# Decoder layer on one core: the last two pipeline steps get orders of their own on TensorE, ScalarE and VectorE

## Chip, cores and metric

The kernel runs on one core of a Trainium2 chip. The metric is the device time of one execution in microseconds, the median of the runs shown. Its engines are TensorE (PE, with its weight loads as PEld), VectorE (DVE), ScalarE (ACT), GpSimd (POOL) and SyncE (SP, which issues the large DMAs). Each engine works through its own instructions in the order in which they are written; between engines only semaphores order the work.

## What is computed

Eight batches of 512 tokens with 512 features pass three layers, each followed by a layer norm: a retention (a decaying sum over time, a linear map, a convolution of 5 taps), an mLSTM attention against a context, and a mixture of 32 experts. The part that matters here is the attention's end, the norms behind it, and the router:

```python
# attention, per batch, 8 heads of 64
log_D = cs[:, :, None] - cs[:, None, :] + ig[:, None, :]      # masked: lower triangle
D_mat = jnp.exp(log_D - max_log_D)
C = qk * D_mat
normalizer = jnp.maximum(jnp.abs(C.sum(-1, keepdims=True)), jnp.exp(-max_log_D))
h = jnp.einsum('hst,htd->hsd', C / (normalizer + EPS), vh)
h = layernorm(h) * ln_scale
x = layernorm(x + h)
# router, over all 4096 tokens
ri = jnp.concatenate([xf, stats(xf)], -1)     # stats: mean, std, min, max, l2, share of tiny values
h = jax.nn.gelu(ri @ r1_w.T + r1_b, approximate=False)
probs = jax.nn.softmax(h @ r2_w.T, -1)
topp, topi = jax.lax.top_k(probs, 2)
idx = jnp.argsort(-score, axis=0)[:cap].T     # each expert takes its 160 best of ALL tokens
```

Because each expert picks its tokens from all batches, nothing of the experts can start before the router's result of the last batch.

## The kernel before

**The pipeline.** The first third of the time is a software pipeline over the eight batches. `run_pipeline` calls `step` for n = 0 to 9 on each engine. In step n three things are interleaved: batch n's retention, first norm and gates (flag `a`, n < 8), batch n-1's attention (flag `s`), and batch n-2's two norms and router (flag `r`). So step 8 (`n.off == NB`) has the attention of batch 7 and the norms and router of batch 6, and no batch of its own; step 9 has only the norms and router of batch 7. The order is written out by hand in one `step` per engine, for TensorE, ScalarE, VectorE and GpSimd; steps 8 and 9 use the same list with the missing parts left out.

**Attention of a batch**, by pairs of heads j = 0 to 3. TensorE `broadcast_max(b, h)` (L545 on, two bf16 matmuls, L556 and L557) writes a head's maxima to the bank `Bb`; ScalarE `decays(b, h)` (L1017) takes their exponential into `Dm[h // 2 % 2]`, and waits for `values` of the pair that used that buffer before, two pairs back. TensorE `scores(b, j)` (L656) makes q times k; VectorE `weigh(b, j)` (L1233) multiplies them into `Dm`. `broadcast_decay(b, j)` (L567) also writes `Bb`, and VectorE `scale_queries(b, j)` (L1242) reads it. TensorE `values(b, j)` multiplies by the values (L672) and adds the earlier chunks' state (L683); VectorE `head_out(b, j)` (four small operations and L1293) divides and writes to `x2`. Since `Bb` is one bank, every broadcast waits for the reader of the one before.

**Norms and router of a batch.** VectorE `norm2_stats` (L1300 to L1308), `norm3_sum` (L1316) and `norm3_stats` (L1323, L1327), with a power on GpSimd after the first (`rstd2`) and after the last (`shift3`); ScalarE `norm3_out` (L933), then `squares` (L943); TensorE `router_in` transposes the four tiles (L700), ScalarE `router_1` copies them out (L1031); VectorE `router_extreme` (L1378), `router_sparse` (L1369) and `router_stats` (L1385 to L1390); GpSimd `roots`; TensorE `router_stats` (L712), `router_hidden` (L718), `router_hidden_stats` (L723); ScalarE copies (L1037) and the Gelus `router_2` (L1042); TensorE `router_logits` (L730); ScalarE `router_3` copies the logits (L1047); VectorE `softmax_1` (L1395, L1397) subtracts the maximum; ScalarE `router_4` takes the exponential (L1052); VectorE `softmax_2` and `top_two` (L1402 to L1433) end with the semaphore step `save`. The selection behind it (DVE L1538 on) waits for `save` of batch 7.

The last lines of the steps on ScalarE and VectorE are these:

```python
                if r:
                    router_4(n - 2)          # ScalarE, L1123: waits for softmax_1 of the same batch
...
                if r:
                    softmax_1(n - 2)         # VectorE, L1516
                if a:
                    weigh(n, 0)
                if n.off == NB + 1:
                    softmax_2(n - 2)
                    top_two(n - 2)
```

`softmax_2` and `top_two` of a batch otherwise come one step later, behind the third norm's statistics. GpSimd's `selection_tables` (L1845 on), constants for the selection, stand at the end of step 8 behind `roots`.

## Time and profile before

| | |
|---|---|
| median of 3 runs | 1753.62 us (1751.96 to 1753.97) |
| profiled execution | 1756.21 us, span on the core 1754.4 us, mean granted clock 0.926 |
| busy over the span | PE 86%, PEld 66%, DVE 43%, ACT 28%, POOL 18% |
| step 8 | from about 545 to 597 us of the span |
| step 9 | 597 to 640.5 us |
| selection and lists | 640.5 to about 750 us |
| experts | about 750 us to the end |

Times in the trace are us from the span's start, and durations us, unless marked ns. A row of the timeline merges successive instructions of one kind (x4: four of them); the bracket at its end gives how long the engine had been idle before and what released it. The ends of matmuls are modelled. PEclk is the granted clock of TensorE as a share of 2.4 GHz: 0.50 is 1.2 GHz.

### The profile page before, as it was taken

Reading aid. Unit: us, or ns where it says so; the run is one execution under the profiler, and the core shown is the slowest. Engines: PE = TensorE matmul, PEld = TensorE weight load, DVE = VectorE, ACT = ScalarE, POOL = GpSimd, SP = SyncE. Lnnn points to the kernel's source line nnn. Section 1 sums busy time; section 2 is a strip of 40 time slices with the busy share of each in tenths; the row PEclk is TensorE's granted clock in tenths of the full one; section 3 lists DMA queues with packets and bytes.
Section 4 is the critical chain, followed back from the end, with each engine's and each line's share of the span. In section 5 each row is a group of like instructions: output and inputs, shape, how many; then the busy total and the mean of one; then the engine's idle time right before and its main releaser. Section 6 shows DMA issues by size and latency. Waiting matters only on the chain.

```text
span 1754.4 us, 28619 instructions
## 1 busy us (share of the span) xinstructions
PE 1504.7 (86%) x11038; PEld 1158.6 (66%) x11076; DVE 758.7 (43%) x1783; ACT 486.9 (28%) x1165; POOL 309.4 (18%) x399
## 2 busy tenths in 40 slices
PE   3589999899897540389999999999999999999995
PEld 2256656556555420278787888878788887878884
DVE  7458999999978569811111111111111111111143
ACT  3446666676664220011111110111111011111123
POOL 3101121111111200011121212112121211212125
PEclk9698998998997765589999999999999999999998
DMA  5203123133211054046776767676776767677696
GB/s 156 72 1 115 48 79 104 48 90 95 75 49 49 1 202 169 0 156 214 285 246 259 264 222 282 214 283 240 264 264 226 278 215 278 239 271 257 230 344 209
DMA packets 92191, 311.02 MB, mean 177 GB/s; under 512 B 42455, under 2 KB 46557, under 8 KB 82781
## 3 DMA queue, kind: packets, MB, share of 16 engines
q1 hardware_dynamic: 78876, 287.87, 44.8%
q0 software_dynamic: 13248, 22.29, 5.6%
q8 instruction: 39, 0.64, 0.1%
q14 instruction: 28, 0.22, 0.0%
HBM read 273.18 MB, written 36.96 MB: 177 GB/s over the span
## 4 chain that ended last, share of the span: by engine, by line
PE 71%; DVE 18%; issue 6%; ACT 3%; DMA 1%; POOL 1%; SPq 0%; DVEq 0%; POOLq 0%; ACTq 0%
PE bank L869 36%; PE banks L881 15%; PE bank L582 5%; PE banks L884 4%; DVE arena L1212 3%; DVE arena L1587 2%; PE banks L672 2%; PE bank L718 1%; PE bank L584 1%; DVE arena L1202 1%; PE banks L683 1%; PE banks L656 1%; DVE arena L1378 1%; PE bank L642 1%; DVE arena L1233 1%
## 5 line engine op out<-in xcount | busy, mean ns | idle before, releaser
L869 PE MATMUL bank<-arena 128*128 128x160 f32 x4608 | 636.0, 300 | 0.7 <-issue 0.7
L869 PEld LDWEIGHTS bank<-arena 128*128 128x128 f32 x4608 | 628.3, 191 | 7.3 <-issue 7.3
L1144 ACT ACTIVATE arena<-bank 128x160 f32<-128x160 f32 x288 | 87.4, 303 | 835.2 <-PE bank L869 835.2
L1748 DVE TENSOR_TENSOR arena<-arena,bank 128x160 f32<-128x160 f32 x256 | 82.3, 322 | 459.4 <-ACT arena L1144 408.8
L881 PE MATMUL banks<-arena 128*128 128x512 f32 x576 | 255.6, 598 | 8.9 <-DVE arena L1750 8.9
L1914 POOL DMA_INDIRECT acc_rows<-arena,keep x64 | 102.8, 1606 | 651.9 <-DVE arena L1693 634.1
L881 PEld LDWEIGHTS banks<-arena 128*128 128x128 f32 x576 | 106.9, 190 | 138.6 <-issue 132.5
L1691 DVE TENSOR_SCALAR arena<-banks,keep 128x512 f32<-128x512 f32 x32 | 24.0, 750 | 318.8 <-PE banks L884 316.6
L582 PE MATMUL bank<-arena 128*128 128x512 f32 x256 | 121.7, 620 | 30.8 <-DVE arena L1212 30.8
L582 PEld LDWEIGHTS bank<-arena 128*128 128x128 f32 x256 | 49.8, 200 | 85.1 <-issue 77.1
L1212 DVE SCALAR_TENSOR_TENSOR arena<-arena 128x512 f32<-128x512 f32 x128 | 96.1, 750 | 3.4
L1017 ACT ACTIVATE arena<-bank,arena 128x128 f32<-128x128 f32 x256 | 72.5, 370 | 43.1 <-PE bank L557 43.1
L884 PEld LDWEIGHTS banks<-arena 128*32 128x32 f32 x2304 | 60.9, 110 | 24.3 <-issue 24.3
L672 PE MATMUL banks<-arena 128*128 128x96 f32 x512 | 71.6, 300 | 2.3 <-DVE arena L1293 2.3
L672 PEld LDWEIGHTS banks<-arena 128*128 128x128 f32 x512 | 68.7, 214 | 7.2 <-issue 7.2
L1902 POOL DMA_INDIRECT arena<-x_rows,keep x64 | 64.2, 1003 | 36.4 <-POOL keep L1894 26.6
L884 PE MATMUL banks<-arena 128*32 128x128 f32 x2304 | 69.5, 274 | 0.0
L1894 POOL COPY keep<-keep 128x2 int32 (+1 forms) x64 | 29.3, 458 | 204.9 <-DVE keep L1682 119.3
L718 PE MATMUL bank<-arena 128*128 128x512 f32 x128 | 60.7, 618 | 0.7 <-ACT arena L1031 0.7
L814 PE MATMUL bank<-arena 128*128 128x1 f16 x30 | 5.6, 185 | 59.2 <-DVE arena L1587 59.2
L1130 ACT ACTIVATE arena<-banks 128x512 f32<-128x512 f32 x32 | 19.1, 597 | 118.7 <-PE banks L850 114.9
L718 PEld LDWEIGHTS bank<-arena 128*128 128x128 f32 x128 | 23.9, 197 | 30.9 <-issue 29.5
(252 smaller groups left out, 1632.9 us busy)
## 6 DMA issues: line engine op xcount, KB each, us to landing
arena<-in_wup SPq DMA_DIRECT2D x32, 4096.0 KB, 12.5
arena<-in_wdn SPq DMA_DIRECT2D x32, 2048.0 KB
arena<-in_aup SPq DMA_DIRECT2D x32, 512.0 KB, 11.7
arena<-in_xT SPq DMA_DIRECT2D x8, 1024.0 KB, 5.3
arena<-in_kT SPq DMA_DIRECT2D x8, 1024.0 KB, 7.2
arena<-in_v SPq DMA_DIRECT2D x32, 256.0 KB, 7.8
x_rows<-arena SPq DMA_DIRECT2D x8, 1024.0 KB, 4.4
acc_rows<-arena SPq DMA_DIRECT2D x8, 1024.0 KB, 6.7
```

The source lines that it names most:

```text
L582: pe.matmul(w[:, :], ST[b.slot][:, c, rows], WT[:, c, :], start=(c == 0), stop=False)
L672: pe.matmul(Pp[:, r * T + tb * PVN:r * T + (tb + 1) * PVN], Dm[j % 2][:, r * T + tb * P:r * T + (tb + 1) * P], va[b.slot][:, tb, h * VW:h ...
L718: pe.matmul(Wb[k][:, :], r1x[:, c, k * P:(k + 1) * P], x2T[:, c, :], start=(c == 0), stop=False)
L869: m = pe.matmul(u[:, g * CAP:(g + 1) * CAP], w, xeT[:, c, :], start=(c == 0), stop=(c == C - 1))
L881: m = pe.matmul(Yb[0][:, :], hact[:, j, 0:P], w, start=(j == 0), stop=(j == J))
L884: m = pe.matmul(Yb[1][CAP2 * c:CAP2 * (c + 1), 0:P], hact[:, j, P:CAP], w[:, c * P:(c + 1) * P], start=(j == 0), stop=(j == J))
L1017: m = act.activation(d[:, tb * P:(tb + 1) * P], Bb[:, tb * P:(tb + 1) * P], ACT.Exp, bias=gcol[b.slot][:, tb, h:h + 1])
L1144: act.activation(sg[k], Ub[k][:, 0:CAP], ACT.Silu).then_inc(up_a(f"silu{j}"), 1)
L1212: dve.scalar_tensor_tensor(row, xT[:, c, k:k + T], cw[:, c, k:k + 1], row, ALU.mult, ALU.add).then_inc(re_v(f"tap{i}_{c}"), 1)
L1748: dve.tensor_tensor(hact[:, j, :], sg[k], u, ALU.mult).then_inc(up_v(f"mul{j}"), 1)
L1902: pool.indirect_dma_start(out=xg[e.slot][:, cols], out_offset=None, in_=rows, in_offset=bass.IndirectOffsetOnAxis(ap=idx_g[e.slot][:, k:k ...
L1914: pool.indirect_dma_start(out=rows, out_offset=bass.IndirectOffsetOnAxis(ap=idx_s[e.slot][:, k:k + 1], axis=0), in_=yy[e.slot][:, cols], i ...
```

## The change

Steps 8 and 9 get lists of their own, `last_values` (step 8, on TensorE, ScalarE and VectorE) and `last_rows` (step 9, VectorE). In step 8 the scores of pair 1 come ahead of the decay and the values of pair 0, the broadcasts and values of batch 7 come ahead of batch 6's router on all three engines, and batch 6's hidden layer and logits come behind `values(b, 3)`. VectorE does batch 6's `norm3_sum` and `norm3_stats` between parts of the attention, and its extremes, counts and statistics around `head_out(b, 3)`. Batch 5's `softmax_2` and `top_two` and batch 6's `softmax_1` move from step 8 to step 9, behind the statistics of batch 7's third norm; batch 6's `softmax_2` and `top_two` go behind batch 7's `router_stats`. On ScalarE, batch 5's `router_4` moves from the end of step 7 to behind `decays(b, 3)`; batch 6's `router_4` is the last of step 8. A 1-element activation on a new tile `tab` with the function Gelu, and one with Exp, stand ahead of the places in steps 8 and 9 where the tables change. In step 9 TensorE does both halves of `router_hidden` ahead of `router_stats`. GpSimd's `selection_tables` move from the end of step 8 to its beginning. The semaphore steps of `softmax_1` move from `ro_v` to `so_v`, since their order among the others is now different.

```diff
@@ -277,6 +277,7 @@
         wsum = room.take(TB)
+        tab = room.take(2)[0:1, 0:1]
@@ -329,9 +330,8 @@
         ro_a = steps("router_scalar", [f"x{tb}" for tb in range(TB)] + ["st", "h0", "h1", "lg", "exp"])
-        ro_v = steps("router_vector", ["extr0", "extr1", "cnt", "msq", "var", "stats",
-                                       "lmax", "lsub"])
-        so_v = steps("softmax_vector", ["lsum", "lrec", "prob", "top", "at",
+        ro_v = steps("router_vector", ["extr0", "extr1", "cnt", "msq", "var", "stats"])
+        so_v = steps("softmax_vector", ["lmax", "lsub", "lsum", "lrec", "prob", "top", "at",
                                        "sum2", "rec2", "oh", "ohs", "save"])
@@ -731,8 +731,38 @@
+            def last_values(b, p):
+                broadcast_max(b, 2)
+                broadcast_max(b, 3)
+                scores(b, 1)
+                broadcast_decay(b, 0)
+                broadcast_max(b, 4)
+                values(b, 0)
+                broadcast_max(b, 5)
+                scores(b, 2)
+                broadcast_decay(b, 1)
+                broadcast_max(b, 6)
+                values(b, 1)
+                broadcast_max(b, 7)
+                broadcast_decay(b, 2)
+                scores(b, 3)
+                broadcast_decay(b, 3)
+                values(b, 2)
+                router_in(p, False, (0, 1))
+                values(b, 3)
+                router_in(p, False, (2, 3))
+                router_hidden(p, 0)
+                router_hidden(p, 1)
+                router_stats(p, False)
+                router_hidden_stats(p)
+                router_logits(p)
             def step(n, a, s, r, x1, x2):
+                if n.off == NB:
+                    last_values(n - 1, n - 2)
+                    return
                 if s:
@@ -782,8 +812,11 @@
                 if r:
+                    if n.off > NB:
+                        router_hidden(n - 2, 1)
                     router_stats(n - 2, a)
-                    router_hidden(n - 2, 1)
+                    if n.off < NB:
+                        router_hidden(n - 2, 1)
                     router_hidden_stats(n - 2)
@@ -1022,11 +1055,12 @@
-            def router_1(b, before):
-                act.wait_ge(*ro_t.at("h1", b - 1))
-                if before:
-                    act.wait_ge(*n1_a.at(f"out{TB - 1}", b + 2))
-                for tb in range(TB):
+            def router_1(b, before, tiles=range(TB)):
+                if tiles[0] == 0:
+                    act.wait_ge(*ro_t.at("h1", b - 1))
+                    if before:
+                        act.wait_ge(*n1_a.at(f"out{TB - 1}", b + 2))
+                for tb in tiles:
                     act.wait_ge(*ro_t.at(f"x{tb}", b))
@@ -1043,16 +1077,41 @@
                 act.wait_ge(*ro_t.at("lg", b))
-                act.wait_ge(*ro_v.at("lsub", b - 1))
+                act.wait_ge(*so_v.at("lsub", b - 1))
                 act.activation(lg, Wb[0][:, 0:TB * NE].rearrange("p (a e) -> p a e", a=TB), ACT.Copy)\
...
+            def table(f):
+                act.activation(tab, tab, f)
+            def last_values(b, p):
+                decays(b, 2)
+                decays(b, 3)
+                router_4(p - 1)
+                for h in range(4, NH):
+                    decays(b, h)
+                norm3_out(p)
+                router_1(p, False, (0, 1))
+                squares(p)
+                router_1(p, False, (2, 3))
+                table(ACT.Gelu)
+                router_stats(p)
+                router_2(p, 0)
+                router_2(p, 1)
+                table(ACT.Exp)
+                router_3(p)
+                router_4(p)
             def router_4(b):
-                act.wait_ge(*ro_v.at("lsub", b))
+                act.wait_ge(*so_v.at("lsub", b))
                 act.activation(pr, pr, ACT.Exp).then_inc(ro_a("exp"), 1)
...
+                if n.off == NB:
+                    last_values(n - 1, n - 2)
+                    return
                 if s:
@@ -1097,6 +1156,8 @@
                     gates_1(n)
+                if n.off > NB:
+                    table(ACT.Gelu)
                 if r:
@@ -1110,12 +1171,14 @@
                     gates_g(n)
+                if n.off > NB:
+                    table(ACT.Exp)
                 if r:
...
                     first_state(n)
-                if r:
+                if r and n.off != NB - 1:
                     router_4(n - 2)
@@ -1170,7 +1233,7 @@
-            for t in (xT[:, :, 0:PAD], xT[:, :, PAD + T:], wgq, wgk, wgv, gm, Fr[0], Fr[1], stT, r1s, bfs[0], bfs[1], zeros):
+            for t in (xT[:, :, 0:PAD], xT[:, :, PAD + T:], wgq, wgk, wgv, tab, gm, Fr[0], Fr[1], stT, r1s, bfs[0], bfs[1], zeros):
                 dve.memset(t, 0.0)
@@ -1392,10 +1455,10 @@
                 dve.wait_ge(*so_v.at("save", b - 1))
-                dve.tensor_reduce(nmx, lg, AX.X, ALU.max).then_inc(ro_v("lmax"), 1)
-                dve.wait_ge(*ro_v.at("lmax", b))
+                dve.tensor_reduce(nmx, lg, AX.X, ALU.max).then_inc(so_v("lmax"), 1)
+                dve.wait_ge(*so_v.at("lmax", b))
                 dve.tensor_tensor(pr, lg, nmx.unsqueeze(2).to_broadcast([P, TB, NE]), ALU.subtract)\
-                    .then_inc(ro_v("lsub"), 1)
+                    .then_inc(so_v("lsub"), 1)
@@ -1436,8 +1499,53 @@
+            def last_values(b, p):
+                norm2_stats(p)
+                scale_queries(b, 0)
+                weigh(b, 1)
+                norm3_sum(p)
+                head_out(b, 0)
+                scale_queries(b, 1)
+                norm3_stats(p)
+                weigh(b, 2)
+                head_out(b, 1)
+                scale_queries(b, 2)
+                weigh(b, 3)
+                scale_queries(b, 3)
+                head_out(b, 2)
+                router_extreme(p, 0)
+                head_out(b, 3)
+                router_extreme(p, 1)
+                router_sparse(p)
+                router_stats(p)
+            def last_rows(b):
+                norm2_stats(b)
+                norm3_sum(b)
+                norm3_stats(b)
+                softmax_2(b - 2)
+                top_two(b - 2)
+                softmax_1(b - 1)
+                router_extreme(b, 0)
+                router_extreme(b, 1)
+                router_sparse(b)
+                router_stats(b)
+                softmax_2(b - 1)
+                top_two(b - 1)
+                softmax_1(b)
+                softmax_2(b)
+                top_two(b)
             def step(n, a, s, r, x1, x2):
+                if n.off == NB:
+                    last_values(n - 1, n - 2)
+                    return
+                if n.off == NB + 1:
+                    last_rows(n - 2)
+                    return
                 if r:
@@ -1516,9 +1624,6 @@
                     weigh(n, 0)
-                if n.off == NB + 1:
-                    softmax_2(n - 2)
-                    top_two(n - 2)
@@ -1863,6 +1968,8 @@
+                if n.off == NB:
+                    selection_tables()
                 if r:
@@ -1879,8 +1986,6 @@
                     gate_chunks(n)
-                if n.off == NB:
-                    selection_tables()
```

## Rows read from the trace of the kernel before

**Rows 1.** Stages: length; busy PE, PEld, DVE, ACT, POOL; granted clock; DMA share, GB/s.
```profile
545.00:597.20 52.20, 39.52 (x228) 28.99 (x230) 34.10 (x92) 19.37 (x51) 10.62 (x27) 0.77 0.11 41
597.20:640.60 43.40, 17.61 (x57) 9.73 (x57) 26.45 (x90) 13.21 (x28) 6.11 (x9) 0.67 0.13 49
```

**Rows 2.** VectorE's timeline, step 8: start, us, operation, [idle <-releaser].
```profile
549.23 2.74 DVE L1308 SCALAR_TENSOR_TENSOR arena<-arena 128x512 f32<-128x512 f32 x4
...
554.66 0.55 DVE L1242 TENSOR_TENSOR arena<-arena,bank 128x384 f32<-128x384 f32 x1
...
565.33 4.47 DVE L1378 TENSOR_REDUCE arena<-arena 128x4 f32<-128x2048 f32 x2
...
572.48 0.17 DVE L1390 TENSOR_SCALAR arena<-arena 128x4 f32<-128x4 f32 x1
...
595.62 0.17 DVE L1284 SCALAR_TENSOR_TENSOR arena<-banks,arena 128x8 f32<-128x8 f32 x1 [3.02 <-PE banks L683]
...
596.47 0.69 DVE L1293 TENSOR_TENSOR arena<-banks,arena 128x512 f32<-128x512 f32 x1
```

**Rows 3.** ScalarE's timeline at the start of step 8 and inside it.
```profile
545.30 0.31 ACT L1052 ACTIVATE arena<-arena 128x128 f32<-128x128 f32 x1 [4.42 <-DVE arena L1397]
...
557.82 1.14 ACT L1017 ACTIVATE arena<-bank,arena 128x128 f32<-128x128 f32 x4 [9.07 <-PE bank L557]
```

**Rows 4.** TensorE's timeline in step 8, at either clock.
```profile
564.75 2.08 PE L656 MATMUL banks<-arena 64*128 64x128 f32 x16
566.76 3.73 PE L672 MATMUL banks<-arena 128*128 128x96 f32 x16
570.41 1.55 PE L683 MATMUL banks<-arena 64*128 64x65 f32 x12
...
572.30 0.63 PE L557 MATMUL bank<-arena 128*128 128x512 bf16 x1
...
592.75 2.00 PE L672 MATMUL banks<-arena 128*128 128x96 f32 x16
594.69 0.89 PE L683 MATMUL banks<-arena 64*128 64x65 f32 x12
```

**Rows 5.** Stretches of 4 us (columns as in Rows 1).
```profile
568.00:572.00 4.00, 4.00 (x25) 3.71 (x25) 4.00 (x8) 0.00 (x0) 0.00 (x0) 0.50 0.45 167
...
620.00:624.00 4.00, 3.38 (x6) 1.11 (x4) 2.77 (x12) 0.00 (x0) 1.18 (x2) 0.75 0.16 60
```

**Rows 6.** GpSimd's timeline in step 8.
```profile
549.28 0.79 POOL L1807 TENSOR_SCALAR arena<-arena 128x4 f32<-128x4 f32 x1 [18.50 <-DVE arena L1304]
...
575.37 3.68 POOL L1771 TENSOR_SCALAR_AFFINE_SELECT arena<-arena 128x128 f32<-128x128 f32 x10
```

**Rows 7.** VectorE's timeline, step 9 and the end of the router.
```profile
597.60 2.46 DVE L1300 BATCH_NORM_STATS2 arena<-arena 128x6 f32<-128x512 f32 x4
...
608.57 0.38 DVE L1327 BATCH_NORM_AGGREGATE arena<-arena 128x2 f32<-128x6 f32 x4
...
614.22 4.48 DVE L1378 TENSOR_REDUCE arena<-arena 128x4 f32<-128x2048 f32 x2 [1.57 <-ACT arena L933]
...
636.72 0.29 DVE L1402 TENSOR_REDUCE arena<-arena 128x4 f32<-128x128 f32 x1 [1.01 <-ACT arena L1052]
...
640.22 0.29 DVE L1433 TENSOR_TENSOR keep<-arena 128x128 f32<-128x128 f32 x1
```

**Rows 8.** ScalarE's timeline, step 9.
```profile
610.89 0.81 ACT L933 ACTIVATE arena<-arena 128x512 f32<-128x512 f32 x1 [12.87 <-POOL arena L1819]
...
630.16 1.28 ACT L1042 ACT_TABLE_LOAD   x1 [3.76 <-PE bank L723]
```

**Rows 9.** TensorE's timeline, step 9.
```profile
617.44 5.94 PE L718 MATMUL bank<-arena 128*128 128x512 f32 x8 [0.69 <-ACT arena L1031]
625.18 0.60 PE L712 MATMUL bank<-keep,arena 128*6 128x128 f32 x4 [1.80 <-issue]
625.62 3.61 PE L718 MATMUL bank<-arena 128*128 128x512 f32 x8
```

## Prediction

> **What bounds the kernel now.** I read the busy time by stage first. In step 8 TensorE is busy 39.5 of 52.2 us at a mean clock of 0.77, VectorE 34.1; in step 9 TensorE is busy 17.6 and VectorE 26.5 of 43.4 [rows 1]. No engine is full in either: both are chains of one batch across four engines, so it is the order of the chain that counts. Behind step 9 stands the selection, which waits for `save` of batch 7 at 640.51 (the end of the last of rows 7), and the experts wait for it in turn. No operation behind `save` is changed, so what `save` gains or loses, the kernel gains or loses. The forecast is therefore one number: when `save` of batch 7 comes.
>
> Then the timelines of each engine, followed backwards from `save`. Step 9 is batch 7 alone and cannot start before its `head_out(b, 3)` at 597.16, which had waited 3.02 us for TensorE [rows 2]; the reader is to see there that in step 8 TensorE does batch 6's hidden layer and logits ahead of batch 7's last values. The change takes that work off batch 7's way in step 8 and puts other work on its way in step 9. I lay out both chains.
>
> **Step 8, laid out anew.** It starts where VectorE ends `norm2_stats(6)`, at 551.97 [rows 2]; this is the same in both kernels. ScalarE has by then no debts: at the end of step 7 it sat 4.42 us waiting for batch 5's `softmax_1` before its exponential [rows 3]. With `router_4` moved behind `decays(b, 3)`, both decays are done by about 544.9 in place of 548.8, but VectorE is in `norm2_stats` until 551.97 anyway, so this gain is hidden; it is worth nothing at the end.
>
> Prices, from rows. At the low clock: a broadcast is two matmuls of 512 columns, L557 at 0.63 and one ahead of it that it overlaps by half: 0.95; scores 2.08, 2.0 on the chain; values from 566.76 to 571.96, 5.15 on the chain [rows 4]. At the high clock: values from 592.75 to 595.58, 2.8 [rows 4]. A decay broadcast is one matmul of three quarters of the columns of L557, hence 0.5 [rows 4]. Decays of one head 1.14 [rows 3], `scale_queries` 0.55 and `head_out` from 595.62 to 597.16, 1.54 [rows 2]. Each hand-over costs some 0.05, which I put into the items.
>
> I take the low clock from the start, because TensorE stands idle for most of the stretch in which VectorE does `norm2_stats(6)`. The new list then gives a chain that hardly ever waits for VectorE's norms: `scale_queries(0)` to 552.5; broadcast 4 to 553.5; values 0 to 558.65; decays 4 (they need the buffer that values 0 frees) to 559.85; broadcast 5, scores 2, decay broadcast 1 to 563.3; `scale_queries(1)` to 563.85; broadcast 6 to 564.8; values 1 to 569.95; decays 6, broadcast 7, decays 7 to 573.25; decay broadcast 2, scores 3, decay broadcast 3 to 576.2; values 2 to 581.35. All of VectorE's `norm3_sum`, `norm3_stats` and `weigh` lie beside it. Then `router_in(p, False, (0, 1))`, which stands between values 2 and values 3: two tiles of transposes, at most 2.0 since they are eight matmuls of the width of scores. That is 583.35. Values 3 costs 2.8 or 5.15; TensorE has worked since 573.3 with almost no break, and before it rose in such a stretch, so I take 3.4: 586.75. `head_out(b, 3)` ends at 588.3, against 597.16: **8.9 us earlier**. With 5.15 for values 3 it is 590.05.
>
> **What now stands on batch 7's way.** (1) VectorE does `router_extreme(p, 1)`, `router_sparse(p)` and `router_stats(p)` of batch 6 between `head_out(b, 3)` and `norm2_stats(7)`: half of 4.47, plus the rest up to the end of the last statistic at 572.65, 2.85 [rows 2]: +5.1 us. Before, only `softmax_1(6)` stood there, from 597.16 to 597.60: -0.45. (2) The three norm pieces take 11.35 (597.60 to 608.95) [rows 7] in both. (3) Before, ScalarE began `norm3_out(7)` at 610.89, 1.94 behind 608.95, released by GpSimd's `shift3` [rows 8]. Now `router_4(6)` stands ahead of it on ScalarE's queue. It waits for `softmax_1(6)`, and that stands on VectorE behind `softmax_2(5)` and `top_two(5)`, 3.8 us (the same operations for batch 7: 636.72 to 640.51) [rows 7]. So `norm3_out(7)` starts 3.8 + 0.65 + 0.35 = 4.8 behind the third norm in place of 1.94: **+2.85 us**. This is the new wait of this change: everything behind `router_4(6)` on ScalarE is held, first `norm3_out(7)`, and for that wait TensorE's transposes and VectorE's extremes. Of batch 5's softmax only the 1.94 us of GpSimd's work lie in cover.
>
> Sum to the start of `norm3_out(7)`: 588.3 + 5.1 + 11.35 + 4.8 = 609.55, against 610.89: **1.35 us earlier**.
>
> **The tail of step 9.** Before, statistics were ready for TensorE at 625.18 (L712), and the second half of the hidden layer came behind them [rows 9]. The first half takes 5.94, partly at the low clock; the second, at the high clock, 3.6 [rows 9]. Both halves first, on the old time axis: from 617.44 they end at 626.9, so L712 goes then and not at 625.18. It takes 0.5; ScalarE's copy of its 512 columns takes at most the 0.81 of an activation of that size [rows 8], say 0.6; and half of L723, two matmuls of 512 columns where a hidden half has eight in 3.6, takes 0.9. The first Gelu's input stands at 629.0, against 630.16 when ScalarE left its wait for it [rows 8]: **-1.15 us**. The Gelu table load of 1.28 [rows 8] goes into ScalarE's wait for statistics: before it had idled 3.76 us right ahead of the load [rows 8] and more ahead of that: **-1.3**. If that cover were gone, 1.28 would be back on the path. The Exp table load ran beside `softmax_1` and held the exponential for part of VectorE's 1.01 us wait at 636.72 [rows 7]; the exponential itself is 0.31 plus hand-overs, so **-0.65**; it now lies beside the logits. Batch 6's `softmax_2` and `top_two` (3.8) lie between `router_stats(7)` and `softmax_1(7)`, a stretch in which VectorE waits some 10 us for TensorE and ScalarE: nothing. Together -3.1. If the first half of the hidden layer meets a clock that is already high, up to 1 more.
>
> A rule of the Trainium skill on the tables: in our rows the load is 1.28 and the first Gelu follows at once [rows 8]. The Trainium skill, "ScalarE: Activation LUTs", section "What ACT_TABLE_LOAD costs", puts a switch of sets at about 2.66 us, since it counts a drain of 1.38 with the load. By the page the two preloads would hide up to 1.4 us more each; no row here shows such a drain on the path, and the sum goes by 1.28.
>
> **Edits at nothing.** `selection_tables` first in step 8: the ten selects that make most of it take 3.68 us, and GpSimd had stood idle 18.5 us before `rstd2(6)` at 549.28 [rows 6]; the tables wait only for batch 7's decay rows, ready by then, so they end near 545.5. If they were late, `rstd2(6)` would hold `norm3_sum(6)`, which now has 2 us of slack behind `weigh(b, 1)`. The stores of batch 6's rows start some 13 us later than at 563, those of batch 7 a little earlier; nobody waits for them before the selection. One more `memset` of one element at the start: under 0.1. The renamed semaphore steps cost nothing.
>
> **Sum.** -1.35 - 3.1 = -4.45, or -5.45 with a first hidden half at the high clock; errors of hand-overs are about 1 either way. I take -5.3, because the hand-laid chain, put to the old order in the same way, comes out about half a us later than the trace. On the profiled execution of 1756.21 that is 1750.9; that execution lies 2.6 above the median of the runs, so on the median it is **1748.3**.
>
> **The rivals.** *Early high clock.* What TensorE's clock does in step 8 is the largest open term. TensorE worked from 568 to 572 without a pause, all value products, at 0.50 [rows 5]; in hidden-layer matmuls of 512 columns the clock went up inside 620 to 624 (0.75) [rows 5]. The new list has broadcasts and scores in a row at 559.9 to 563.3; if the clock rises there or one run of values later, values 1 and 2 save 2.35 each, the broadcasts, scores 3 and transposes about 2.2, values 3 another 0.6: about -7.5 on top, **1740.8**. For it: fewer long pauses from 559.9 on than before. Against it: pauses of 1.1 us at every decay, and half the time is value products, during which it stayed low.
>
> *Low to the end.* The clock stays low through values 3, and hand-overs cost a bit more, or a preload does not take its load off the path (the change doing less than it says; 1.3 and 0.65). Then `head_out(b, 3)` ends at 590.05 and the sum is -4.45 + 1.75 = -2.7, and without the Gelu preload -1.4; I name the middle: **1751.5**, within 0.2%.
>
> *The other batch's router comes late* (slower than before). `router_4(6)` holds `norm3_out(7)` until the logits of batch 6 are there. In my layout these are copied at about 602 to 603, and VectorE asks for them at 609.2: 6.5 us of slack. If the clock also stays low through both hidden halves, they take about 6.9 each (5.94 with a part at the high clock [rows 9]) from 592 on, and end at 606; statistics, L723 and logits at the low clock take 10 more: 616. `norm3_out(7)` then starts at 617.1, 6.2 later than before; less the tail's 3.1, +3.1: **1756.7**. It decides from logits later than 609.2 on. Against it: the row in which just these matmuls raised the clock [rows 5]. The Trainium skill, "TensorE: Matmul & The Clock Gate", section "Part 1: The HAM clock gate (the "warmup" mystery)", has a clock that is halved after idling and comes back after sustained work; by that rule an order that splits TensorE's work into short pieces with waits between them, as this one does at every decay, speaks against the change. The row of 568 to 572 shows more than the page says: even unbroken work left it low.
>
> **How the numbers follow.** The forecast 0.60 (its own range 1746.3 to 1750.5), early high clock 0.22, low to the end 0.14, late router 0.04. About 0.2%, 3.5 us, is what a measurement of this kernel can tell from no change. Faster by more: all of the early clock and nine tenths of the forecast, 0.76, and 0.02 of the third, 0.78; within: 0.18; slower: 0.04. The range must keep the early clock's middle and the third case: 1740.5 to 1751.5.
>
> **What the profile after would show.** `head_out(b, 3)` of batch 7 ending near 588 (582 with the early clock); VectorE's extremes, counts and statistics between it and the second norm, 5.1 us; `norm3_out(7)` released by the exponential of batch 6 (or by VectorE's L1397) and no longer by GpSimd, 4.8 behind the third norm; no table load between L723 and the Gelus of step 9; the exponential of batch 7 right behind `softmax_1`; `save` near 635; everything behind it as long as before. I am wrong if the selection or the first expert takes longer in reaction, if TensorE's clock path differs, or if ScalarE's queue blocks elsewhere.

## The result and the profile after

| | before | changed kernel |
|---|---|---|
| median | 1754.4 us (20 runs) | 1751.87 us (20 runs) |
| ratio to the kernel before | | 0.998, 95% interval 0.997 to 0.9989 |
| profiled execution | 1756.21 us, span 1754.4 | 1749.58 us, span 1747.7 |

The forecast was -5.3 us and 1748.3, from a median before of 1753.62. The ratio says -3.5 us, between -1.9 and -5.3, which on that median is 1750.1; the two medians of the table, taken as they stand, differ by 2.5. In the two profiled executions the span is 6.7 us shorter. Two slow executions are left out of the ratios: one of the kernel before beside b1 and b2 (1797.68 us at a mean clock of 0.886) and one of the six of b2 (2380.34 us at 0.732). The page of the changed kernel (span; busy time, share and count of each engine; the chain of waits by engine) is almost the old one; the gain is not to be seen in shares:

```profile
span 1747.7 us, 28624 instructions
...
PE 1506.6 (86%) x11038; PEld 1159.1 (66%) x11076; DVE 758.2 (43%) x1784; ACT 488.8 (28%) x1169; POOL 309.9 (18%) x399
...
PE 70%; DVE 20%; issue 5%; ACT 3%; DMA 1%; POOL 0%; SPq 0%; DVEq 0%; POOLq 0%; another core or an unknown queue 0%; ACTq 0%
```

The timeline of VectorE in the changed kernel answers to rows 2 and 7. In order: `weigh(7, 0)`, with which I let step 8's chain begin in all kernels; `head_out(7, 0)`; the end of `head_out(7, 3)`; the first extreme after it; the first and the last operation of the second and third norm of batch 7; batch 6's `softmax_1`; the extremes of batch 7; the operation that gives `save`.

```profile
544.27 1.22 DVE L1296 SCALAR_TENSOR_TENSOR arena<-banks,arena 128x1024 f32<-128x1024 f32 x1
...
557.50 0.17 DVE L1347 SCALAR_TENSOR_TENSOR arena<-banks,arena 128x8 f32<-128x8 f32 x1 [2.20 <-PE banks L683]
...
584.51 0.69 DVE L1356 TENSOR_TENSOR arena<-banks,arena 128x512 f32<-128x512 f32 x1
...
585.12 2.28 DVE L1441 TENSOR_REDUCE arena<-arena 128x4 f32<-128x2048 f32 x1
...
590.15 2.47 DVE L1363 BATCH_NORM_STATS2 arena<-arena 128x6 f32<-128x512 f32 x4
...
601.12 0.38 DVE L1390 BATCH_NORM_AGGREGATE arena<-arena 128x2 f32<-128x6 f32 x4
...
605.62 0.29 DVE L1460 TENSOR_TENSOR arena<-arena 128x128 f32<-128x128 f32 x1
...
609.48 4.48 DVE L1441 TENSOR_REDUCE arena<-arena 128x4 f32<-128x2048 f32 x2 [3.57 <-ACT arena L966]
...
633.54 0.29 DVE L1496 TENSOR_TENSOR keep<-arena 128x128 f32<-128x128 f32 x1
```

The chip ran the stages in the order that the prediction lays out: after `head_out(7, 3)` (585.20) come 4.95 us of batch 6's statistics, the norms end at 601.50, and the next thing on the way is batch 6's `softmax_1`, not GpSimd's shift. ScalarE's timeline shows this (answer to rows 8): the exponential of batch 6 released by L1460 (`softmax_1`), `norm3_out(7)` right behind it; then the Gelu table load in a wait, the two Gelus, the Exp table load, the exponential of batch 7:

```profile
605.95 0.31 ACT L1108 ACTIVATE arena<-arena 128x128 f32<-128x128 f32 x1 [6.94 <-DVE arena L1460]
...
606.16 0.80 ACT L966 ACTIVATE arena<-arena 128x512 f32<-128x512 f32 x1
...
615.11 1.28 ACT L1085 ACT_TABLE_LOAD   x1
...
625.12 0.69 ACT L1076 ACTIVATE arena<-bank,arena 128x512 f32<-128x512 f32 x1 [1.28 <-PE bank L723]
...
626.69 1.28 ACT L1085 ACT_TABLE_LOAD   x1
...
629.69 0.31 ACT L1108 ACTIVATE arena<-arena 128x128 f32<-128x128 f32 x1 [0.68 <-DVE arena L1460]
```

TensorE's timeline (answer to rows 4 and 9): values 1, values 2, the transposes of two tiles, values 3, then in step 9 both hidden halves in one piece, the statistics, L723.

```profile
563.71 3.57 PE L672 MATMUL banks<-arena 128*128 128x96 f32 x16
...
567.21 1.55 PE L683 MATMUL banks<-arena 64*128 64x65 f32 x12
...
575.08 3.18 PE L672 MATMUL banks<-arena 128*128 128x96 f32 x16
578.18 0.89 PE L683 MATMUL banks<-arena 64*128 64x65 f32 x12
579.00 1.09 PE L700 MATMUL bank<-keep,arena 128*128 128x128 f32 x8
580.80 2.00 PE L672 MATMUL banks<-arena 128*128 128x96 f32 x16 [0.71 <-DVE arena L1356]
582.73 0.89 PE L683 MATMUL banks<-arena 64*128 64x65 f32 x12
...
612.71 10.08 PE L718 MATMUL bank<-arena 128*128 128x512 f32 x16 [0.69 <-ACT arena L1065]
...
622.62 0.60 PE L712 MATMUL bank<-keep,arena 128*6 128x128 f32 x4
...
623.90 1.98 PE L723 MATMUL bank<-arena 128*128 128x512 f32 x4 [0.68 <-ACT arena L1071]
```

Five lengths describe each kernel; all are differences of two rows of its timelines, as those above. "Start" is the start of `weigh(7, 0)`; step 8 goes from there to the end of `head_out(7, 3)`; "norms" to the last statistic of batch 7's third norm; "hold" from there to the start of `norm3_out(7)`; "tail" from its end (3.2 behind its start) to `save`; "sum" from start to `save`.

| kernel | start | step 8 | norms | hold | tail | sum |
|---|---|---|---|---|---|---|
| before | 545.18 | 51.98 | 11.79 | 1.94 | 26.41 | 95.33 |
| changed | 544.27 | 40.93 | 16.30 | 4.66 | 24.47 | 89.56 |
| changed, again (c_after) | 549.17 | 40.86 | 16.29 | 4.67 | 24.43 | 89.44 |
| e1_norm_first | 545.75 | 42.87 | 16.30 | 1.95 | 24.40 | 88.72 |
| e2_no_preload | 548.96 | 43.29 | 16.30 | 4.79 | 24.89 | 92.48 |
| e3_step9_only | 544.60 | 49.87 | 11.79 | 1.94 | 23.59 | 90.40 |
| e4_filler | 543.08 | 31.35 | 16.29 | 4.67 | 24.13 | 79.64 |
| e5_before_filler | 543.73 | 48.05 | 11.79 | 1.94 | 26.41 | 91.40 |
| e6_filler_norm_first | 546.08 | 34.81 | 14.10 | 1.94 | 24.43 | 78.49 |
| e7_filler_all | 544.83 | 32.38 | 14.11 | 1.94 | 22.35 | 74.00 |
| b1_best | 544.14 | 32.36 | 14.11 | 1.94 | 22.33 | 73.95 |
| b2_best_more | 548.10 | 32.36 | 14.11 | 1.94 | 22.57 | 74.19 |

So of the 6.7 us between the two profiled spans, 0.9 came ahead of step 8, where the code is the same, 5.8 from steps 8 and 9, and nothing behind: from `save` to the end of the span it is 1113.89 before and 1113.87 after. Step 8 gives 11.05; the norms' stretch gives back 4.5, the hold 2.7; the tail gives 1.9.

### The profile page after: what moved, and what is told of

The parts are those of the page before. It is cut to its first block, busy times and chain, and to the rows that moved or that the text cites. A ratio compares the mean times of both kernels' runs of the same rounds, so it can differ in the third digit from the quotient of the medians.

```text
span 1747.7 us, 28624 instructions
## 1 busy us (share of the span) xinstructions
PE 1506.6 (86%) x11038; PEld 1159.1 (66%) x11076; DVE 758.2 (43%) x1784; ACT 488.8 (28%) x1169; POOL 309.9 (18%) x399
## 4 chain that ended last, share of the span: by engine, by line
PE 70%; DVE 20%; issue 5%; ACT 3%; DMA 1%; POOL 0%; SPq 0%; DVEq 0%; POOLq 0%; another core or an unknown queue 0%; ACTq 0%
PE bank L902 36%; PE banks L914 15%; PE bank L582 5%; PE banks L917 4%; DVE arena L1275 3%; DVE arena L1692 2%; PE banks L672 2%; DVE arena L1265 1%; PE bank L584 1%; PE bank L718 1%; PE banks L656 1%; PE banks L683 1%; DVE arena L1441 1%; DVE arena L1432 1%; DVE arena L1296 1%
## 5 line engine op out<-in xcount | busy, mean ns | idle before, releaser
L672 PEld LDWEIGHTS banks<-arena 128*128 128x128 f32 x512 | 70.2, 218 | 8.1 <-issue 7.9
L672 PE MATMUL banks<-arena 128*128 128x96 f32 x512 | 72.5, 303 | 3.0 <-DVE arena L1356 3.0
```

The costliest lines, as they stand in the source:

```text
L672: pe.matmul(Pp[:, r * T + tb * PVN:r * T + (tb + 1) * PVN], Dm[j % 2][:, r * T + tb * P:r * T + (tb + 1) * P], va[b.slot][:, tb, h * VW:h ...
```

## Experiments

### Is it ScalarE's queue that holds the norm? (e1)

```diff
             def last_values(b, p):          # ScalarE, step 8
...
                 router_3(p)
-                router_4(p)
...
                 if r:
                     norm3_out(n - 2)
+                if n.off > NB:
+                    router_4(n - 3)
```

> The changed kernel with ScalarE's router_4(6) moved from the end of step 8 to behind norm3_out(7). If the 4.7 us between the third norm's last statistic (601.5) and norm3_out(7) (606.16) in the changed kernel come from router_4(6) standing ahead of it on ScalarE, norm3_out(7) starts 2.0 to 2.2 behind the statistic, released by GpSimd's shift, and save of batch 7 comes 2.4 to 2.7 us earlier than in the changed kernel (some 8.5 earlier than in the kernel before in a profile with the same clock history). Rival: VectorE is the bound there (softmax_2(5), top_two(5), softmax_1(6) end 4.2 behind the statistic, and the extremes cannot start before): then norm3_out starts earlier and save stays within 0.5 of the changed kernel's.

The median was 1750.87, ratio 0.9975 (0.9964 to 0.9985). ScalarE's timeline, `norm3_out(7)` and then the exponential of batch 6:

```profile
606.87 0.81 ACT L966 ACTIVATE arena<-arena 128x512 f32<-128x512 f32 x1 [1.16 <-POOL arena L1925]
...
610.07 0.29 ACT L1107 ACTIVATE arena<-arena 128x128 f32<-128x128 f32 x1
```

The hold falls from 4.66 to 1.95 and the releaser is GpSimd again, as before the change. Step 8 was 1.9 us longer in this execution for another reason (below); with the length of step 8 taken out, the sum is 45.85 against 48.63: 2.8 us, a little more than the 2.4 to 2.7 expected. VectorE was no second bound: it ends `softmax_1(6)` before it needs `norm3_out(7)`. The whole runs do not tell the two kernels apart: 0.9975 (0.9964 to 0.9985) against 0.998 (0.997 to 0.9989).

### What are the preloads worth? (e2)

```diff
-                table(ACT.Gelu)
...
-                table(ACT.Exp)
...
-                if n.off > NB:
-                    table(ACT.Gelu)
...
-                if n.off > NB:
-                    table(ACT.Exp)
```

> The changed kernel without the four 1-element activations. If the preloads pay as in the sum, the table load of Gelu is back between the hidden statistics and the first Gelu in steps 8 and 9, and Exp's behind the logits: step 9 longer by 1.3 + 0.6 = 1.9 us; step 8's loads are in cover and cost nothing at the end. Rival 1 (the Trainium skill's 2.66 us for a switch, if a drain lay on the path too): 4 us. Rival 2 (the loads were hidden before already): 0.

Median 1753.76, ratio 0.999 (0.9978 to 1.0003), against 0.998 (0.997 to 0.9989) with the preloads; the intervals overlap, so the worth is read from the profile. The tail alone (24.89 against 24.47) misleads, because this execution's hidden halves met a better clock. From L723, behind them, it is clean. ScalarE's timeline: the load, the Gelus, the load, the exponential; and TensorE's L723:

```profile
631.10 1.28 ACT L1076 ACT_TABLE_LOAD   x1 [1.26 <-PE bank L723]
...
632.39 1.27 ACT L1076 ACTIVATE arena<-bank,arena 128x512 f32<-128x512 f32 x2
...
636.01 1.28 ACT L1106 ACT_TABLE_LOAD   x1
...
637.31 0.31 ACT L1106 ACTIVATE arena<-arena 128x128 f32<-128x128 f32 x1
```

```profile
629.89 1.98 PE L723 MATMUL bank<-arena 128*128 128x512 f32 x4 [0.68 <-ACT arena L1071]
```

From the start of L723 to `save` it is 641.44 - 629.89 = 11.55, against 633.83 - 623.90 = 9.93 in the changed kernel: 1.6 us, near my 1.95. The missing 0.3 is in the Gelus: with the load ahead of them they ran back to back (1.27 for both), without it the first starts sooner and the second waits for its half of L723 (1.55 from 625.12). The first Gelu starts 0.01 behind the end of the load; the figure of 2.66 us with a drain, from the Trainium skill's "ScalarE: Activation LUTs", section "What ACT_TABLE_LOAD costs", would have made it some 4 us, by the estimate in the expectation. No time of a drain lay on this path.

### Step 9's edits alone (e3)

The kernel before with two edits, both in step 9:

```diff
                 if r:
+                    if n.off > NB:
+                        router_hidden(n - 2, 1)
                     router_stats(n - 2, a)
-                    router_hidden(n - 2, 1)
+                    if n.off <= NB:
+                        router_hidden(n - 2, 1)
...
+                if n.off > NB:
+                    table(ACT.Gelu)
                 if r:
                     router_stats(n - 2)     # ScalarE
...
+                if n.off > NB:
+                    table(ACT.Exp)
                 if r:
                     router_3(n - 2)
```

> The kernel before with step 8 left as it was and two edits in step 9 alone: both halves of the hidden layer ahead of the statistics on TensorE, and the two preloads. By the sum 3.1 us are gained (1.15 order, 1.3 Gelu table, 0.65 Exp table): 0.998 of the kernel before. By the changed kernel's trace its step 9 from norm3_out's end to save was 24.4 against 26.3 before, so 1.9 if the first hidden half has the same clock as there, up to 3 otherwise. Rival: all of the change's gain sits here (then the ratio equals the changed kernel's, 0.998, and step 8's new order is worth nothing).

Median 1752.44, ratio 0.9986 (0.9977 to 0.9995), against 0.998 for the whole change. The intervals overlap: the whole runs do not exclude the rival, that all of the gain sits in step 9 and step 8's new order is worth nothing once the norms and the hold have taken their 7.2 us back. Its tail is 23.59, 2.8 under 26.41. This run also gave what the first two profiles could not: step 8, in which nothing was changed, was 49.87 long in place of 51.98. The stretch of step 8 in one row (length; busy PE, PEld, DVE, ACT, POOL; granted clock; DMA) has as much clock in the mean; what differs is which matmuls got it. In 568 to 572 the clock was 1.00 here and 0.50 in the first profile [rows 5], and values 1 took 3.58 in place of the 5.20 of [rows 4].

```profile
544.60:594.47 49.87, 36.94 (x228) 26.66 (x230) 33.85 (x92) 19.31 (x51) 10.63 (x27) 0.77 0.12 43
```

```profile
566.17 2.76 PE L673 MATMUL banks<-arena 128*128 128x96 f32 x16
568.86 0.89 PE L684 MATMUL banks<-arena 64*128 64x65 f32 x12
```

### Is it the clock that makes step 8 long? (e4, e5)

e4 is the changed kernel with matmuls of no use in TensorE's waits; they write a bank that nobody reads there.

```diff
+            def filler(k):
+                for i in range(k):
+                    pe.matmul(Tb[:, :], identh, upper_h.rearrange("p a t -> p (a t)"), start=True, stop=True)
             def last_values(b, p):          # TensorE, step 8
...
                 broadcast_max(b, 3)
+                pe.wait_ge(*st_v.at("S2", b))
+                filler(6)
                 scores(b, 1)
                 broadcast_decay(b, 0)
+                filler(8)
                 broadcast_max(b, 4)
                 values(b, 0)
+                filler(4)
                 broadcast_max(b, 5)
...
+                filler(1)
                 broadcast_max(b, 6)
                 values(b, 1)
+                filler(3)
                 broadcast_max(b, 7)
+                filler(4)
                 broadcast_decay(b, 2)
```

> The changed kernel with 26 matmuls of 512 bf16 columns of no use in step 8, in TensorE's waits, into a bank that nobody reads then (they add work and change no result). If the low clock is what makes step 8's chain long, the granted clock stays at 1.00 from 543 to head_out(7, 3), values take 2.8 instead of 5.1, and head_out(7, 3) ends 5 to 7 us earlier than in the changed kernel (585.2 there), with the run-to-run spread smaller. Rival: the chain is bound by VectorE and ScalarE hand-overs; then TensorE is faster but only waits longer, and the gain is under 2 us; if the fillers delay the broadcasts, it is slower.

Median 1740.74, ratio 0.9917 (0.9902 to 0.9931): ten microseconds under the changed kernel, from work that computes nothing. Step 8 of the changed kernel and of this one, in a row of the same kind each:

```profile
544.27:585.20 40.93, 29.54 (x186) 24.61 (x188) 25.42 (x55) 12.53 (x37) 4.24 (x7) 0.59 0.14 52
```

```profile
543.08:574.43 31.35, 23.78 (x206) 17.67 (x208) 25.24 (x55) 12.53 (x37) 4.22 (x7) 1.00 0.18 67
```

The granted clock is 1.00 in place of 0.59. Values 1, which took 563.71 to 568.76 above, stands so in TensorE's timeline with fillers:

```profile
558.14 1.92 PE L672 MATMUL banks<-arena 128*128 128x96 f32 x16
...
559.99 0.89 PE L683 MATMUL banks<-arena 64*128 64x65 f32 x12
```

5.05 has become 2.74, scores 1.16 in place of 2.08, and the other stages of the table stand within 0.4. The rival, that hand-overs bind the chain, is out: of the 9.6 us that step 8 lost, values 0 to 2 are 5.9 (two of 2.3 and 1.25 for values 2), and scores 2 and 3 another 1.8. The five executions of e4 lie within 0.9 us (1740.02 to 1740.92), the twelve of the changed kernel (c_after) within 7.7; but e6 and e7, with the same fillers, lie within 4.7 and 4.6, so a smaller spread is not shown to come with them.

e5 puts 29 of the same into the waits of the kernel before: 14 behind the first broadcast of step 8, 5 behind the first decay broadcast, 10 ahead of the second.

```diff
                 if s:
                     broadcast_max(n - 1, 2)
+                if n.off == NB:
+                    pe.wait_ge(*st_v.at("S2", bl))
+                    filler(14)
...
                     broadcast_decay(n - 1, 0)
+                if n.off == NB:
+                    filler(5)
...
+                if n.off == NB:
+                    filler(10)
                 if s:
                     broadcast_decay(n - 1, 1)
```

> The kernel before, with 29 useless matmuls of 512 bf16 columns in TensorE's waits of step 8 (behind the first broadcast, behind the first decay broadcast, ahead of the second). If the low clock is the cost of the old order too, its step 8 falls from 52.0 to some 44 to 46 us and the kernel to about 0.9965; head_out(7, 3) still comes some 10 us later than in the changed kernel with fillers (31.4 us), which would be the worth of the order at the high clock. Rival: the fillers' whole gain of 10 us comes with the old order too; then the order is worth nothing at the high clock and the time is near 1746.

Median 1754.32, ratio 0.9996 (0.9983 to 1.0009): no change that can be told. Step 8 in its row; VectorE's two longest waits in it, for values 2 and values 3; and the first of these in the kernel before:

```profile
543.73:591.78 48.05, 37.34 (x250) 25.34 (x250) 33.68 (x92) 19.31 (x51) 10.62 (x27) 0.93 0.12 45
```

```profile
585.69 0.17 DVE L1296 SCALAR_TENSOR_TENSOR arena<-banks,arena 128x8 f32<-128x8 f32 x1 [7.63 <-PE banks L683]
...
590.25 0.17 DVE L1296 SCALAR_TENSOR_TENSOR arena<-banks,arena 128x8 f32<-128x8 f32 x1 [3.02 <-PE banks L683]
```

```profile
591.06 0.17 DVE L1284 SCALAR_TENSOR_TENSOR arena<-banks,arena 128x8 f32<-128x8 f32 x1 [7.63 <-PE banks L683]
```

The fillers did raise the clock, to 0.93, and in this profile step 8 fell to 48.05, by less than the 44 to 46 expected; but the 7.63 us and 3.02 us for which VectorE waits for TensorE are to the hundredth those of the kernel before (the second in [rows 2]). There TensorE does batch 6's hidden layer and logits ahead of the last values, and it did them at the high clock already. The profiled execution, at 1750.83, is the fastest of e5's twelve (up to 1758.04), so what the profile gains need not hold for the others, and by the median they gained nothing; why is open.

For the order's worth at a high clock the profiles give 48.05 against 31.35 in step 8, 16.7 us, of which norms and hold give back 7.2, and from start to `save` 91.40 against 79.64, 11.8. The whole runs agree in kind: 0.9996 against 0.9917 is 14 us. At the clock that the chip gave by itself, step 8 was 51.98 against 40.93. The new list has the shorter chain, but it moves the hidden layer and the logits, TensorE's densest work of step 8, behind the last values: its mean clock there is 0.59 in place of 0.77. That this move is what kept the clock low is argued, not shown. (My fillers here let the clock drop once, from about 552 to 559, so 48.05 is likely an upper bound.)

### The changed kernel again (c_after)

> The changed kernel itself again, beside the others on one chip, for a second profile. If TensorE's clock in step 8 differs from execution to execution, its step 8 (weigh of pair 0 to head_out(7, 3)) may again differ from the 40.9 us of the first profile by up to 3 us with the same code, while the stretch from head_out(7, 3) to norm3_out(7), 16.3 + 4.7, which has no TensorE on it, stays within 0.2. Rival: the length of step 8 is fixed by the order and comes out at 40.9 again.

Median 1750.91, ratio 0.9982 (0.997 to 0.9994). For these two profiles the rival was right about step 8: 40.86 and 40.93; norms and hold agree within 0.01, as expected. What I had looked for in step 8 sits ahead of it: the start came at 549.17, 4.9 us later than in the first profile of the same kernel. Most of this was lost early: `norm2_stats(1)`, in step 3, starts at 217.47 in the first profile and at 221.61 in this one, 4.1 later. What loses the time there is open.

```profile
217.47 2.46 DVE L1363 BATCH_NORM_STATS2 arena<-arena 128x6 f32<-128x512 f32 x4
```

```profile
221.61 2.47 DVE L1363 BATCH_NORM_STATS2 arena<-arena 128x6 f32<-128x512 f32 x4
```

Over all profiles the start lies between 543.08 and 549.17, with nearly the same code up to there in all but the last kernel (the change moves one exponential and GpSimd's tables, the fillers come with step 8). Yet step 8 is not fixed by its order either: e1 and e2 give TensorE and VectorE the same lists up to `head_out(7, 3)`, and measured 42.87 and 43.29. In e2 the clock rose only inside values 3 (L672 from 586.53 to 589.85, then L683 in 0.89). In e1 values 3 ran at the low clock to its end (3.70 and 1.55). In the row of e1 the mean clock is 0.56, and a high stretch came early, inside values 1, and was lost again:

```profile
545.75:588.62 42.87, 32.70 (x186) 28.01 (x188) 25.43 (x55) 12.20 (x36) 4.24 (x7) 0.56 0.13 49
```

```profile
581.86 3.70 PE L672 MATMUL banks<-arena 128*128 128x96 f32 x16
585.49 1.55 PE L683 MATMUL banks<-arena 64*128 64x65 f32 x12
```

### Toward a faster version (e6, e7, b1, b2)

e6 is e4 with e1's edit and one more, on VectorE:

```diff
                 scale_queries(b, 3)
+                router_extreme(p, 0)
                 head_out(b, 2)
-                router_extreme(p, 0)
+                router_extreme(p, 1)
                 head_out(b, 3)
-                router_extreme(p, 1)
```

> The changed kernel with the fillers of step 8, ScalarE's router_4(6) behind norm3_out(7), and VectorE's two extremes of batch 6 one place earlier (ahead of head_out(7, 2) and head_out(7, 3)). Against the kernel with the fillers alone: 2.7 us for norm3_out(7) not held, 1.1 us net for the extremes (4.5 less behind head_out(7, 3), some 2 to 3.5 given back in the waits before it). About 1737. Rival: the extremes delay head_out(7, 2) and so values 3 by as much as they free; then 2.7 alone.

Median 1737.08, ratio 0.9894 (0.9878 to 0.9911): 3.7 us under e4 by the medians and 4 by the ratios, as expected (3.8). In the profiled execution the fillers lost the clock for some 7 us, so step 8 was 34.81; the norms' stretch fell from 16.29 to 14.10 and the hold to 1.94. In e7, with the same lists on VectorE and the clock at 1.00 throughout step 8, step 8 is 32.38, 1.0 more than in e4, so the extremes' move is worth 2.2 - 1.0 = 1.2.

e7 adds fillers behind batch 6's logits (20), behind batch 7's logits (20 matmuls of `ident`), and 6 of these in each of the 30 rounds of the selection.

```diff
                 router_logits(p)
+                filler(20)
...
             run_pipeline(step)
+            def small(k):
+                for i in range(k):
+                    pe.matmul(Bb[:, 0:P], ident, ident, start=True, stop=True)
+            small(20)
             pe.wait_ge(*so_v.at("save", bl))
...
                 pe.matmul(Tb[:, 0:1], blk_f, cnt, start=True, stop=True).then_inc(se_t(f"cnt{i}"), 1)
+                small(6)
```

> As the kernel with fillers, norm3_out first and earlier extremes, and with useless matmuls also behind batch 6's logits, behind batch 7's logits, and in each round of the selection. If the low clock costs the same way there, the four transposes and the first hidden half of step 9 take 1.1 and 3.6 in place of 2.0 and 5 to 6, worth 2.3 us until the statistics bound it; the first transposes of the selection 0.9; each of the 30 rounds some 0.05 to 0.1 for its one small matmul: 3 to 6 us together, 1731 to 1734. Rival: VectorE bounds the selection's rounds whatever the clock: then 3 us from step 9 alone; or the fillers stand in the way of a matmul that becomes ready (slower).

Median 1738.83, ratio 0.9906 (0.9891 to 0.9922), no better than e6. The tail fell by 2.1 to 22.35, and in the selection the first counting product comes 4.64 behind `save` in place of 5.25. But the last comes at 66.89 in place of 66.53: the 29 rounds between take 62.25 in place of 61.28. The loss of 1.0 us is not spread over the rounds. TensorE's timeline of the first two (the counting product, the fillers behind it):

```profile
623.47 0.16 PE L865 MATMUL bank<-arena 128*128 128x1 f16 x1 [3.48 <-DVE arena L1712]
623.49 2.91 PE L853 MATMUL bank<-keep 128*128 128x128 f32 x12
626.19 0.21 PE L865 MATMUL bank<-arena 128*128 128x1 f16 x1
626.26 2.91 PE L853 MATMUL bank<-keep 128*128 128x128 f32 x12
```

The first two rounds take 2.72 and 2.78 in place of 2.10 and 2.19. The clock had fallen to 0.50 there, and six fillers then take 2.91, longer than a round: the counting product waits for them. The other 27 rounds, nearly all at the high clock, take 56.75 against 56.99 in the changed kernel, so VectorE bounds them whatever the clock, and the fillers in them bring 0.2. That half of my expectation was wrong, and both its rivals were right. By these stages e7 should come out 1.7 below e6; its median lies 1.75 above, inside the spread of both.

b1 keeps e7's fillers outside the rounds, with longer rows in step 8 (6, 14, 5, 1, 4, 4 in place of 6, 8, 4, 1, 3, 4) and 24 ahead of the selection.

> The kernel with fillers in step 8 (34, more of them in the longest wait), norm3_out(7) first, earlier extremes, fillers behind batch 6's logits and ahead of the selection's first transposes, none in the selection's rounds, where they made a round 0.03 us longer. From weigh of pair 0 to save 73 to 74 us (89.5 in the changed kernel, 95.3 before), from save to the first product of the selection 4.6 in place of 5.25, the rounds 61.3 as before: about 1735. Rival: the longer filler row delays the broadcast behind it by 1 to 2 us.

Median 1735.01, ratio 0.9886 (0.9869 to 0.9903): the fastest version, 1.1% under the kernel before. Sum 73.95, the first counting product 4.66 behind `save`, the rounds back at 61.3, all as expected. (The 0.03 us per round in the expectation is the mean over 29 rounds; the loss sat in two of them, as shown above.) Step 8 in its row, and `norm3_out(7)` on ScalarE, once more released by GpSimd:

```profile
544.14:576.50 32.36, 25.52 (x214) 18.46 (x216) 27.35 (x56) 12.51 (x37) 4.22 (x7) 1.00 0.18 66
```

```profile
592.55 0.81 ACT L980 ACTIVATE arena<-arena 128x512 f32<-128x512 f32 x1 [2.49 <-POOL arena L1939]
```

b2 adds 8 fillers at the head of each retention in steps 1 to 7:

```diff
+                w = Wb[tb % 2]
+                if tb == 0 and b.off:
+                    pe.wait_ge(*st_a.at("S0", b - 1))
+                    for i in range(8):
+                        pe.matmul(w[:, :], identh, upper_h.rearrange("p a t -> p (a t)"), start=True, stop=True)
                 pe.wait_ge(*re_v.at(f"tap{TAPS - 2}_{C - 1}", b))
-                w = Wb[tb % 2]
                 if tb == 0:
                     pe.wait_ge(*st_a.at("S0", b - 1))
```

> The same, and 8 useless matmuls of 512 bf16 columns at the head of each step's retention (steps 1 to 7), into the bank that the retention is about to overwrite. If the 6 us by which the start of step 8's attention differs between profiles (543.1 to 549.2) come from clock drops at those waits, the start moves to 543 or below and the median falls by 2 to 4 us; rival: the drops come earlier in a step, behind the logits, so the fillers come too late and only add 8 x 0.22 us where there was no wait: 0 to +5.

Median 1746.94, ratio 0.9945 (0.993 to 0.996), 12 us slower than b1 and beyond the rival's +5. In the profile the start of step 8 is at 548.10, 4 us later than in b1, and steps 8 and 9 are the same within 0.3. The 4 us are lost in the first steps: `norm2_stats(0)`, in step 2, starts at 155.19 in place of 151.41, and from there to step 8 it stays 3 to 5 us behind.
The profiled execution is the fastest of b2 (1738.93; the others lie between 1745.19 and 1747.32), so most lose some 8 us more than this one. Whether that is the fillers' own time in steps that had no wait for them, or a clock history that they made worse, is open.

## Why the prediction was right, and where its steps were off

**The direction, the chain and the two debts** (batch 6's statistics and the hold) were right. The forecast's number was 1748.3, -5.3 us. The ratio gives -3.5 us, 1750.1 on the median that the forecast started from, inside the range of 1740.5 to 1751.5. The median of 1751.87 as it stands lies 0.4 above the range; the kernel before measured 0.8 more beside it than ahead of the prediction. Point by point:

- **Step 8's new chain.** I had `head_out(7, 3)` at 588.3 on the old time axis. It came at 585.20 with everything 0.9 earlier, so at 586.1: 2.2 earlier than laid out. Up to values 1 my chain and the trace agree within 0.3 (569.95 laid out, 568.76 + 0.9 = 569.7 measured); then the clock rose inside values 2 (3.18 for L672 in place of 3.73) and not first in values 3. The term that was mis-sized is values 2, transposes, values 3: 5.15, 2.0 and 3.4 laid out, 10.55 together; 8.54 measured (3.99, 1.1, 2.8, and a wait of 0.7 for `head_out(7, 2)` that the layout did not have). This hangs on the execution: in e2 the clock rose inside values 3, as laid out, and step 8 is 43.29 against 43.1 laid out; in e1 it was low to the end of values 3, with 42.87.
- **What stands on batch 7's way.** Batch 6's statistics: 5.1 laid out, 4.95 measured (585.20 to 590.15). The hold: 4.8 laid out, 4.66 measured, and e1 shows that it is the place in ScalarE's queue that makes it.
- **The tail** was too high: 3.1 laid out, 1.94 measured. The failing term is the order of the hidden halves, laid out at -1.15. The first Gelu starts 15.76 behind `norm3_out`'s end (625.12 - 609.36) and was let go 16.06 behind it before (630.16 - 614.10): -0.3. I had the halves at 5.94 and 3.6, as in the old trace, 9.5 together; L712 could follow only 9.9 behind their start (612.71 to 622.62), since here the clock rose some 6 us into them and before some 4.5, and from L712 to the first Gelu it is 2.5 and not 2.1. In e3, where L712 follows after 9.0, the tail is worth 2.8. The preloads were right in mechanism: 1.95 laid out, 1.6 measured (e2).
- **The median.** By the profiles the change is worth 5.8 in steps 8 and 9, by the ratio 3.5. What both kernels' profiles show can close this: unchanged step 8 was 51.98 and 49.87, the new list's 40.93, 40.86, 42.87 and 43.29. With the means, 50.9 and 42.0, step 8 gives 8.9, norms and hold take 7.2, the tail gives 1.9: 3.6. So the pair of profiled executions was a pair that favoured the change, and my sum, tuned to one trace's clock, inherited it. This is worked out from few profiles; the length of step 8 in the other executions was not seen. By the same means the new list of step 8, less norms and hold, is worth 1.7, about as much as the tail's edits with 1.9.
- **From -4.45 to -5.3.** The chain adds up to -4.45. I moved it to -5.3 on the ground that the layout comes out half a us late; no row of the prediction shows this, and the step is 0.85. Without it the forecast would have been 1749.2, nearer to what came.
- **Low to the end** as a rival, 0.14 at 1751.5: its number is 1.4 from the ratio's 1750.1, the forecast's 1.8. Its clock did occur, in e1's profile, and not in the two of the changed kernel; its preload that does not take its load off the path did not (e2). That the total fell between the two numbers is in part luck: step 8 was faster than laid out in the first profile, the tail slower, and the old step 8 differs by 2.1 between two profiles.
- **Early high clock** as a rival: I gave it 0.22, at 7.5 us on top. In none of the profiles did an early rise hold by itself (e1 had one and lost it); e4 forced it, and it is worth 9.6 in step 8. **Late router**: the logits of batch 6 were copied at 598.73 and asked for at 605.3 (6.3 of slack, 6.5 laid out); it never decided. In e7 and b1, too, GpSimd's shift, not the router, released the norm.
- **Edits at nothing.** GpSimd's tables ended at 544.66, ahead of the 548.37 at which `rstd2(6)` could start; the later stores held nobody, from `save` to the first product of the experts it is 111.39 before and 111.36 after.

## What to carry to other kernels

When a step is moved off one chain, list for each engine's queue what it now stands in front of: here a 0.3 us exponential, last in one step's list, held the next step's norm for 2.7 us. Price a matmul chain at both clocks, and ask of a new order not only how long its chain is but what clock TensorE gets in it (0.59 against 0.77 here); a sum tuned to one execution's clock history is good to a few microseconds at best. In waits that are long and known, matmuls into an unused bank were worth more (10 us) than the whole reordering (3.5 us). In the old order, whose longest waits were for work already done at the high clock, they were worth nothing in the median; in the selection's rounds they cost 1.0 us where they met the low clock, and 8 more in each retention cost 12.

## What the runs showed of the hardware

In the changed kernel TensorE worked from 563.71 to 568.76 on values without a pause, and the granted clock stayed at 0.50, 1.2 GHz; in e1 it rose inside the same values. In e4, 26 matmuls of 512 bf16 columns in the waits held it at 1.00, 2.4 GHz, over the 31 us of step 8, where useful work alone got 0.59 in the mean. The Trainium skill, "TensorE: Matmul & The Clock Gate", section "Part 1: The HAM clock gate (the "warmup" mystery)", says that sustained matmul work brings the high clock; the held clock of e4 agrees, the values row does not show it. A table load took 1.28 us, and the first activation behind it started 0.01 later (e2). And nearly the same code ahead of step 8 took between 543.1 and 549.2 us in eleven executions of ten kernels, and 544.3 and 549.2 in two of one kernel: a spread larger than what the change was worth.
